# Column sums of a softmax as fp16 products of a total split in two, one tile later

## The reference

```
xn  = group_norm(x, 32 groups)
qkv = W_qkv @ xn + b                       # 1x1 convolution, 4 heads of 64 channels
S   = einsum('bhdk,bhdq->bhkq', q, k) / 8  # 4096 x 4096 per head and batch
P   = softmax(S, axis=-1)
x1  = x + W_proj @ einsum('bhkq,bhdq->bhdk', P, v) + b_proj
y   = relu(batch_norm(x1)); y = conv3x3(y, mean|w0| * sign(w0))
y   = conv3x3(relu(batch_norm(y)), mean|w1| * sign(w1)) + x1
```

## Time and profile before

| | |
|---|---|
| median of the runs | 2705.71 us |
| the profiled execution | 2705.33 us, span 2703.5 us |
| PE busy | 97% of the span |
| VectorE (DVE), GpSimd (POOL), ScalarE (ACT) busy | 80%, 75%, 61% |
| granted clock of TensorE | 0.99 of full speed |
| attention, blocks and stages | 97 us to 2331 us |
| GpSimd's totals of blocks 1 and 2 start at | 227.25 us, 290.77 us |
| convolutions | 2332 us to the end |

### The profile page before, as it was taken

One profiled execution on the slowest core, in us unless ns is written; L12 is line 12 of the kernel. 1 busy time (PEld: TensorE's weight loads), 2 busy tenths in 40 slices (PEclk: granted clock), 3 DMA queues, 4 the chain that ended last, 5 costly groups with the idle time before them and its releaser, 6 DMA issues. The chain is left out here.

```text
span 2703.5 us, 73165 instructions
## 1 busy us (share of the span) xinstructions
PE 2611.3 (97%) x31180; PEld 1175.6 (43%) x31180; DVE 2169.0 (80%) x2796; ACT 1659.8 (61%) x2597; POOL 2024.6 (75%) x1164
## 2 busy tenths in 40 slices
PE   4999999999999999999999999999999999799898
PEld 2444444445444444444444444454444444344343
DVE  7788888758888888577888887688888884888785
ACT  4666666776666667746666667766666666244432
POOL 2799999986999999857999999779999997000122
PEclk9999999999999999999999999999999999899999
DMA  5100000002000000041000000000000000621022
GB/s 220 62 2 2 2 2 2 2 2 69 2 2 2 2 2 2 2 158 54 2 2 2 2 2 2 5 29 2 2 2 2 2 2 2 194 69 48 32 93 93
DMA packets 26941, 79.92 MB, mean 30 GB/s; under 512 B 1920, under 2 KB 2304, under 8 KB 25600
## 3 DMA queue, kind: packets, MB, share of 16 engines
q1 hardware_dynamic: 25648, 73.01, 7.8%
q10 hardware_dynamic: 976, 2.37, 0.3%
HBM read 58.60 MB, written 16.78 MB: 28 GB/s over the span
## 5 line engine op out<-in xcount | busy, mean ns | idle before, releaser
L615 POOL TENSOR_TENSOR acc_pool<-acc_pool,prob 128x1024 f32<-128x1024 f32 (+1 forms) x960 | 1718.4, 1790 | 154.1 <-ACT prob L681 24.6
L681 ACT ACTIVATE prob<-ps,exp_scale 128x512 f32<-128x512 f32 x2048 | 1295.9, 684 | 642.7 <-PE ps L913 642.7
L1006 DVE TENSOR_REDUCE m_part<-ps 128x2 f32<-128x1024 f32 x1024 | 1247.8, 1225 | 268.5 <-PE ps L869 179.8
L895 PE MATMUL ps<-prob,vals 64*64 64x512 f32 x8192 | 1048.5, 590 | 0.0
L907 PE MATMUL ps<-q_hi,k_hi 64*64 64x512 f16 x4096 | 398.2, 377 | 10.3 <-ACT prob L681 8.5
L913 PE MATMUL ps<-m_rows,shift 64*64 64x512 f16 x4096 | 397.1, 376 | 0.0
L907 PE MATMUL ps<-q_lo,k_hi 64*64 64x512 f16 x4096 | 397.0, 376 | 0.0
L907 PE MATMUL ps<-q_hi,k_lo 64*64 64x512 f16 x4096 | 397.0, 376 | 0.0
L1099 DVE TENSOR_TENSOR ps<-ps,prob 128x512 f32<-128x512 f32 x480 | 331.6, 691 | 78.3 <-ACT prob L681 78.3
L895 PEld LDWEIGHTS ps<-prob,vals 64*64 64x64 f32 x8192 | 294.0, 133 | 185.5 <-issue 24.7
L907 PEld LDWEIGHTS ps<-q_hi,k_hi 64*64 64x64 f16 x4096 | 117.0, 104 | 574.0 <-ACT prob L681 534.7
(11 more groups left out here) (134 smaller groups left out, 1687.9 us busy)
## 6 DMA issues: line engine op xcount, KB each, us to landing
xt<-in_x SPq DMA_DIRECT2D x32, 512.0 KB, 4.5
xf<-in_x SPq DMA_DIRECT2D x4, 2048.0 KB, 16.4
xn<-in_x SPq DMA_DIRECT2D x16, 512.0 KB, 7.9
x_scratch<-y_tile SPq DMA_DIRECT2D x16, 512.0 KB, 5.2
rows<-x_scratch SPq DMA_DIRECT2D x8, 576.0 KB, 5.1
rows<-x_scratch SPq DMA_DIRECT2D x8, 544.0 KB, 4.6
xt<-x_scratch SPq DMA_DIRECT2D x4, 1024.0 KB, 5.1
y_tile<-x_scratch SPq DMA_DIRECT2D x4, 1024.0 KB, 5.0
```

What stands on the lines that cost most here:

```text
L615: nc.gpsimd.tensor_tensor(acc[:, part], acc[:, part], tile[:, part], ALU.add).then_inc(pool_add, 1)
L681: nc.scalar.activation(prob[:, n % PBUF, h * TB:(h + 1) * TB], g.ps[:, score_bank(it, kt, h)], ACT.Exp, scale=g.exp_scale[:]).then_inc(exp ...
L895: last = mm(into[own[h], :], vals[keys, kt, own[h]], prob[keys, n % PBUF, h * TB:(h + 1) * TB], start=(kt == 0), stop=(kt == KT - 1))
L1006: v.tensor_reduce(m_part[:, block % 2, :, u], source, AX.X, ALU.max).then_inc(mx_used, 1)
```

## The change

The fp32 product of the total is replaced by two fp16 ones, of its high and of its low part. ScalarE makes the high part (`copy_total`, behind the exponentials of tile 2), VectorE the low part (`split_total`, behind the maxima of tile 3). Both lie in a buffer that the staging of q and k uses otherwise. The sums are taken at tile 5 instead of 4, ahead of the values of tile 0; the division moves to tiles 6 to 13, VectorE's halves to 14 to 27, and their copy to tile 29.

```
-SUMS_AT = LAG
+SUMS_AT = LAG + 1
+TOTAL_AT = LAG - 2
-HALF_AT = KT - 4
+HALF_AT = KT - 3
-DVE_HALVES = list(range(13, 27))
+DVE_HALVES = list(range(14, 28))
-DIVIDE_AT = {LAG + 1 + part: part for part in range(NP)}
+DIVIDE_AT = {SUMS_AT + 1 + part: part for part in range(NP)}
+        ones16 = sb("ones16", [P, HD], F16)
+        tot = y32[:, 0].rearrange("p a n -> p (a n)").bitcast(F16)
+        tot_hi, tot_lo = tot[:, 0:2 * TB], tot[:, 2 * TB:4 * TB]
...
@@ GpSimd, sums, kt == 1
                             pool.wait_ge(sum_ready, it - 1)
+                            pool.wait_ge(tot_lo_ready, it - 1)
@@ ScalarE, softmax, behind the exponentials of kt
+                    if kt == TOTAL_AT and sums_left(it):
+                        copy_total(it - 1)
...
+            def copy_total(it):
+                act.wait_ge(tot_ready, it + 1)
+                if it:
+                    act.wait_ge(sum_ready, it)
+                nc.scalar.activation(tot_hi, acc_pool[:, it % 2], ACT.Copy).then_inc(tot_hi_ready, 1)
...
+            nc.scalar.activation(ones16[:], g.ones[:, 0:HD], ACT.Copy).then_inc(ident_ready, 1)
@@ ScalarE, before a pair's staging
+                    if it0 and hp == 0:
+                        act.wait_ge(sum_ready, it0)
@@ TensorE, column_sums
-                pe.wait_ge(tot_ready, it + 1)
-                for h in range(2):
-                    last = mm(g.ps_misc[own[h], :], g.ones[:, 0:HD], acc_pool[:, it % 2, h * TB:(h + 1) * TB],
-                              start=True, stop=True)
+                pe.wait_ge(tot_lo_ready, it + 1)
+                for part in (tot_hi, tot_lo):
+                    for h in range(2):
+                        last = mm(g.ps_misc[own[h], :], ones16[:], part[:, h * TB:(h + 1) * TB],
+                                  start=part is tot_hi, stop=part is tot_lo)
@@ VectorE
+            def split_total(it):
+                dve.wait_ge(tot_hi_ready, it + 1)
+                v.tensor_tensor(tot_lo, acc_pool[:, it % 2], tot_hi, ALU.subtract).then_inc(tot_lo_ready, 1)
...
                     maxima_of(it0, units_of(qb, kt))
+                    if kt == TOTAL_AT + 1 and sums_left(it):
+                        split_total(it - 1)
```

More of the change, by code:

```diff
@@ L501, in attention @@
         tot_ready = sem("tot_ready")
+        tot_hi_ready, tot_lo_ready = sem("tot_hi_ready"), sem("tot_lo_ready")
         sum_ready = sem("sum_ready")
@@ L700, in softmax @@
                     copy_output(it)
+                    if not sums_left(it + 1):
+                        copy_total(it)
+            def copy_total(it):
[3 more added lines that the diff above has]
+                nc.scalar.activation(tot_hi, acc_pool[:, it % 2], ACT.Copy).then_inc(tot_hi_ready, 1)
             def copy_half(it):
@@ L873, in max_rows @@
             def max_rows(it, into):
-                pe.wait_ge(ident_ready, 1)
+                pe.wait_ge(ident_ready, 2)
                 pe.wait_ge(m_neg_ready, it + 1)
@@ L1130, in query_block @@
                     add_upper(it)
+                    if not sums_left(it + 1):
+                        split_total(it)
             def residual(b, n2, s):
```

## The result

The kernel after takes **2820.35 us** (median of 5 runs, 2817.24 to 2821.24), the kernel before 2705.25 (5 runs beside them). The ratio is 1.042, 95% interval 1.041 to 1.043: 4.2% slower, where 2814.4 was forecast. Its profiled span is 2818.5 us, 115.0 more than before's 2703.5.

A forecast was written before the change was run, and what follows sets the result against it. TensorE was taken to bound the attention loop without gaps, ScalarE and GpSimd right beside it. Terms 51.4 + 51.2 + 3.5 + 2.4 + 0.2 = 108.7 us on 2705.7 gave 2814.4 us, range 2752 to 2845.

The forecast's parts named there:

- The products: Column sums on TensorE: fp16 products with the turn take 0.58 us instead of 1.01, a gain of 0.43 per call.
- rival B: Column sums: the fp16 products don't overlap, 13 us more, 2827 us in all; chance 0.07.
- ScalarE's 1.83: Tiles without values: TensorE waits for a bank freed by ScalarE's exponential, so such a tile takes at least 1.83 us.
- Tile 4: Sums moved behind tile 5's maxima: tiles 4 and 5 together go from 4.16 to at least 4.46 us.
- The subtraction: VectorE's low part, after tile 3's maxima, waits out GpSimd's second addition: +2.14 us in each of 24 middle blocks.
- The late half: VectorE's last half addition, now in iteration 28, and m_neg waiting for GpSimd's addition delay tile 30's maxima: +1.83 us in 28 blocks.
- Is GpSimd in step?: At tile 28: GpSimd catches up with the exponentials by half a microsecond; otherwise m_neg waits less, 0.6 to 1.8 us in all.
- Rival A: VectorE's order costs, but GpSimd doesn't interfere: +1.16 x 24, +0.62 x 28, 2752.5 us; chance 0.27 including the one-wait-only form.
- First and last blocks: Sums: first blocks of second head pairs +1.7 us each, 3.5 total; four last blocks 0 to 1.3, taken 0.6, 2.4 total.
- the start: One more small ScalarE copy at the kernel's start, on the way to the first products: 0.2 us.

The follow-up runs named there:

- e6: Kernel before with the fp32 sums moved to tile 5 and the division to tiles 6 to 13, nothing else; 2726.11 us.
- e7: Kernel before with fp16 products on stand-in data (false sums) at tile 5, no copy and no subtraction; 2713.26 us.
- e3: Kernel before with four fp16 products on stand-in data (false sums) in the old place, tile 4, no copy or subtraction; 2703.43 us.
- e12: e3 with m_neg written by ScalarE and one more half tile on VectorE (13 to 27, copied behind tile 29); 2695.32 us.
- e10: Kernel after with the low part made by two 128x512 VectorE operations with a PSUM operand (false low part), m_neg still on VectorE; 2780.54 us.
- e2: Kernel after with the late half undone: VectorE's half tiles back at 13 to 26, their copy behind tile 28; 2740.45 us.
- e4: Kernel before with VectorE's halves at 14 to 27, copied behind tile 29, and m_neg written by ScalarE except in a pair's first block; 2704.39 us.
- e1: Kernel before with only VectorE's half tiles moved to 14 to 27 and their copy behind tile 29; 2749.17 us (2733.48 to 2759.15).
- e11: e2 with one more half tile on VectorE (12 to 26), so GpSimd has 1.07 us less per block; 2821.97 us.

## Why the prediction was right, and where it was off

- **The products**, 0.58 forecast, 0.55 measured: rival B is out, and behind m(5) the gain is real (e6 against e7, 0.46 a block). In their old place only 0.24 of the 0.43 can arrive, as ScalarE's 1.83 holds s(5), a bound that the forecast had and didn't set against this gain; e3 and e12 show that m_neg and GpSimd decide whether even that does. In the kernel after the products stand in the chain from m(5) to s(6), and there the gain arrives.
- **Tile 4**, 4.16 to at least 4.46: e6 and e7 bear it out (+20 and +7 us); s(4) to s(6) is 4.62 in e7.
- **The subtraction**, "+2.14 us in each of 24 middle blocks": s(4) to s(6) went from 4.16 to 6.25, +2.09. It waited for GpSimd's second addition, as written. By e10 0.93 of that is the wait, by e2 1.1 the order.
- **The late half**, "+1.83 us in each of 28 blocks": the wait of m_neg was forecast from 279.93 to 281.91, 1.98 us, and is 2.00. Where it held, it held to 0.1. e4 shows that it is the whole cost.
- **"Is GpSimd in step?"**, the weakest link. It was, in nearly all blocks of the kernel after: it was to be free 3.4 us behind s(0), and is free 3.35 behind it (372.97, less the 1.16 idle, against 368.46). In the parts alone it wasn't always: e1 in half of its profiled pairs, e2 in none. So 35 us for the sums and 44 for the late half don't make 115. Each half delays TensorE, GpSimd catches up, and then both of VectorE's instructions meet a fresh addition. The prediction's sum was of the state that only both edits together hold; it gives none of the parts.
- **Rival A** failed in the whole change, and was right for e2 (1.1 for its 1.16). Its 0.62 for the late half is refuted by e1 and e4: without GpSimd in the way it is nothing.
- **First and last blocks**: the first blocks of the second head pairs have 3.4 us at the sums, as forecast. A pair's last block gets no longer but 0.2 to 0.3 shorter: the subtraction meets no addition there (1.23 us). In e2 it meets one (2.28 us), and the last blocks cost 1.4 each, near the 1.3 that was the upper end.

The size agrees by errors that nearly cancel, and that is luck. The starts of the scores in the two profiled executions give the whole difference of 115.0 us, term by term:

| us in the kernel | forecast | measured |
|---|---|---|
| sums and subtraction, 24 middle blocks | 51.4 | 51 |
| late half, 28 blocks | 51.2 | 44 |
| sums, first blocks of the second head pairs | 3.5 | 3.4 |
| last blocks of a pair | 2.4 | -1.1 |
| the start | 0.2 | 0.3 |
| TensorE's clock | none | 17 |

Not foreseen at all was **the clock**: 10 blocks at 1.45 to 1.65 us and 1.6 in the first block, read from the totals (69.05 against 67.46) and from m(5) to s(6) (3.32 against 1.80). Without it the kernel after would stand near +98, where the terms give 108.7. Of the 7 us that the late half falls short, 3.4 are the third pair's, whose first two blocks weren't in step (its totals begin 64.50 and 67.87 apart), 2.6 those of the block ahead of a pair's last, where it costs 1.2 and not 1.83, and the rest blocks in which m(30) was late by 0.2 or 0.3 before the change already.

## What to carry to other kernels

A small instruction of VectorE between SBUF tiles can cost as much as is left of the GpSimd instruction that it meets (m_neg 2.0 us here instead of 0.17): before adding or moving one, find GpSimd's addition that runs at that moment, and give the work to ScalarE or a PSUM operand where it lies ahead of what TensorE waits for. Where two engines exclude each other, the price of an edit depends on their phase, and an edit elsewhere, even one that takes work off one of them, can shift it; parts must be measured together. A gain on the busiest engine has to be set against every other loop of about the same length, here ScalarE's tile of 1.83 us and GpSimd's block of 63.5, before it is counted.

## What the runs showed of the hardware

- The phase of two engines can take two courses. One kernel, e1, ran two pairs of heads at +1.8 us a block and two at +0 in one execution, and its runs differ by 26 us, where other kernels' differ by 0.5 to 4. Two pairs of seven blocks at 1.8 would be 25 of them; the slower executions weren't profiled. In the kernel after the third pair went over into step within two blocks.
- TensorE's granted clock fell to the lower level behind waits that are short beside the work. In the kernel after TensorE had waited 1.7 us at m(30), 0.58 at tile 5 and 1.54 at m(5) within 17 us. In the next block the same waits (1.68, 0.58, 1.54) left the clock at 1.00, and in e10, with 1.67 and 0.61, it fell in no block; in e11 2.29 did it each time. A single wait of 2.05 us in the first block did it too, and in e10 one of 2.03 in the same place didn't. What decides between equal waits stays open.
- Four fp16 products, two 64-column halves side by side with a high and a low part each, take 0.55 us with the turn back to 64-row tiles, against 1.01 for the two fp32 ones.
